# Gathering embedding rows straight into the residual tensor, five batches ahead

## The chip, the cores and the metric

One NeuronCore of a Trainium2 chip runs the whole program. The metric is device time in microseconds (us), the median of several runs. TensorE multiplies matrices, VectorE and ScalarE work on tiles, GpSimd does elementwise work and issues the indirect transfers (gathers and scatters by index), and SyncE issues plain transfers.

## The reference

The model is a small early-fusion network over a batch of 16. An image of 96 by 96 is cut into 36 patches and projected to 64 channels; 512 text tokens are looked up in a table of 50257 rows and get a position table added. The 548 tokens then pass four residual blocks, and only the text lookup is touched by this change:

```
h = patches(x) @ tok_W.T + tok_b                       # 16 x 36 x 64
h = concat([h, txt_W[x_txt] + pe], axis=1)             # 16 x 548 x 64
h = h + attn0(layernorm(h))     # relu attention, a two-layer FFN, layer norm
h = h + moe_top1(layernorm(h))  # gate, capacity, expert of 256 hidden units
h = h + attn1(layernorm(h))     # 16 heads of 4 channels, linear attention
h = h + moe_top2(layernorm(h))  # two of 8 experts
```

## The kernel before

Tokens lie on the 128 partitions, five slots of 128 a batch: slots 0 to 3 are the 512 text tokens, slot 4 the 36 image tokens. `H` (128 x 16 x 5 x 64, fp32, in SBUF) is the residual tensor of all 16 batches, and stays there for the whole program. The image slots of `H` are filled once, during the opening, by TensorE and ScalarE (L1070).

The first half of the program (up to the end of the gating of the first expert layer, about 350 us) is a software pipeline over batches. `for step in range(STEPS)` runs on every engine, with 25 steps, and a stage with lag k works on batch `step - k`:

```
LAG = dict(gather=0, norm1=1, cut1=2, qkv=3, attn=4, resid=5, ffn2=6, norm3=7, gate=8, scatter=9)
```

Each engine executes its own part of the step in a fixed order, written out by hand, and waits on semaphores in between; nothing reorders it at run time. What matters around the change:

- GpSimd, per step: `gather(b)` (four indirect transfers of 128 rows of 256 bytes each, L807, one for each text slot, into one of two staging tiles `emb`), then `low1` (L828, the low part of the split of the normalised tile), `offset` (L823, adds a bias row to `H[:, b]`), `scatter` (L815, five indirect transfers), and `low3` (L833). At step 10, ahead of the rest, stand two large subtractions of weights (L840). `gather(b)` from the third batch on waits until the addition that reads the staging tile of batch b - 2 is done.
- VectorE, per step: `norm1a(b)` waits for the gathers of its batch, adds the position table `pe` and writes `H[:, b, 0:4]` (L1307), then takes statistics (L1213, L1216). `norm1b(b)` (L1318 to L1322) normalises into the single tile `xt`, and for b >= 1 first waits for `low1(b-1)`, which reads `xt`. `late_weights(0)` (L1281 to L1295) prepares weights at step 3. `q_low` (L1330) and `k_low` (L1336) follow the projections.
- ScalarE: `roots1` (L1078, L1079) follows `norm1a`; `high1(b)` (L1085) follows `norm1b(b)` and releases `low1(b)`.
- TensorE: at step 3 it runs `moe_bias` (L997) and then `t1(0)` (L852), which waits for `low1(0)`; then the query projection (L862, L863), whose result `q_low(0)` reads before the key projection may begin.
- SyncE issues the weight loads and then 8 transfers of zeros into the scatter buffer, which keep the DMA engines full during the first 45 us.

So `low1(0)`, in step 2, comes behind the twelve gather instructions of steps 0, 1 and 2; `low1(1)` comes in step 3, and so on.

Of the kernel before, what the change touches and what calls it, by code (L numbers as in the profile page):

```python
# [9 lines left out]
ALU = mybir.AluOpType  # L10
# [4 lines left out]
P = 128  # L15
NB, N_IMG, N_TXT, D = 16, 36, 512, 64
# [3 lines left out]
TXT = N_TXT // P  # L20
# [19 lines left out]
PER = dict(norm1a=11, norm1b=4, qk_low=3, vals=1, resid=2, norm2a=12, norm2b=5, norm3a=10, norm3b=3, gate=6, place=7,  # L40
           mixed=12, weighted=5, norm4=5, kvnorm=3, fold=3, resid2=11, norm5=6, route_a=10, route_b=6)
# [37 lines left out]
def early_fusion_kernel(nc, i, out):  # L79
    with ExitStack() as ctx:  # L80
        def sb(name, shape, dt=F32):
            return ctx.enter_context(nc.sbuf_tensor(name, shape, dt))

        def pair(name, shape, dt=F32, depth=2):
            return [sb(f"{name}{k}", shape, dt) for k in range(depth)]
# [3 lines left out]
        def sem(name):  # L89
            if name not in sems:  # L90
                sems[name] = ctx.enter_context(nc.semaphore(name))
            return sems[name]
# [11 lines left out]
        H = sb("H", [P, NB, SLOTS, D])  # L104
# [8 lines left out]
        w = {}  # L113
# [17 lines left out]
        top_w, kept = sb("top_w", [P, NB, SLOTS]), sb("kept", [P, NB, SLOTS])  # L131
        carry = sb("carry", [P, E])

        emb = pair("emb", [P, TXT, D])
        stats = sb("stats", [P, SLOTS, 6])
        mv1, mv2, mv3 = (pair(f"mv{k}_", [P, SLOTS, 2]) for k in (1, 2, 3))
        sd1 = pair("sd1_", [P, 2, SLOTS])
# [33 lines left out]
        def bs(a, k):  # L171
            return a.unsqueeze(1).to_broadcast([a.shape[0], k, a.shape[1]])
# [13 lines left out]
        LAG = dict(gather=0, norm1=1, cut1=2, qkv=3, attn=4, resid=5, ffn2=6, norm3=7, gate=8, scatter=9)  # L186
        STEPS = NB + LAG["scatter"]
        WEIGHTS_STEP = 9

        def at(step, stage):  # L190
            b = step - LAG[stage]
            return b if 0 <= b < NB else None
# [96 lines left out]
        def pool_second(pool):  # L289
# [19 lines left out]
            def finish(b):  # L309

                for side, (_, _, s0, s1) in enumerate(PARTS):
                    pool.wait_ge(sem("weigh"), 2 * (POS * b + (side + 1) * E // 2))
                    h = H[:, b, s0:s1, :]
                    for k in range(2):
                        pool.tensor_tensor(h, h, acc[b % 2][:, s0:s1, k, :], ALU.add).then_inc(sem("finish"), 1)  # L315
                        pool.wait_ge(sem("finish"), 4 * b + 2 * side + k + 1)
# [24 lines left out]
        def pe_second(pe):  # L341
# [60 lines left out]
            def up(n, *tiles):  # L402

                b, side, p = unit(n)
                a, z, _, _ = PARTS[side]
                if n % POS == 0 and 0 in tiles:
                    pe.wait_ge(sem("xs5"), b + 1)
                for k in tiles:
                    j, e = k // 2, 2 * p + k % 2
                    m = up_bank(4 * n + k)  # L410
                    banks.take(pe, (m,), sem("gelu"), 4 * n + k + 1)
                    two(pe, bank(m)[:, 0:z - a], split["fw1"], xs2[b % 2][:, a:z], slice((e * J + j) * P, (e * J + j + 1) * P)).then_inc(sem("up"), 1)
# [356 lines left out]
        @block.sync  # L769
        def _(sp):  # L770
            for n in EARLY[:EARLY_BY_SP]:
                sp.dma_start(w[n][:], i[n]).then_inc(sem("early_in"), 16)
            sp.dma_start(fw1, i["fw1"]).then_inc(sem("middle_in"), 16)
            for n in MIDDLE:
                sp.dma_start(w[n][:], i[n]).then_inc(sem("middle_in"), 16)
            sp.dma_start(ew1, i["ew1"]).then_inc(sem("late_in"), 16)
            for n in LATE:
                sp.dma_start(w[n][:], i[n]).then_inc(sem("late_in"), 16)

            sp.wait_ge(sem("zero_set"), 1)  # L780
            for e in range(E):
                sp.dma_start(slots_buf[e * CP:(e + 1) * CP, :].rearrange("(p t) c -> p t c", p=P), zeros[:].unsqueeze(1).to_broadcast([P, ET, 2 * D])).then_inc(sem("slots_zeroed"), 16)
            for k in range(4):
                sp.wait_ge(sem(f"scattered{k}"), 16 * SLOTS * NB // 4)
            for e in range(E):
                if e >= 2:
                    sp.wait_ge(sem("b_turn"), UE * (e - 1))
                else:
                    sp.wait_ge(sem("low_w"), 2)
                sp.dma_start(xl[e % 2][:], slots_buf[e * CP:(e + 1) * CP, :].rearrange("(p t) c -> p t c", p=P)).then_inc(sem(f"xl_in{e % 2}"), 16)  # L790
                if e >= 2:
                    store_expert(sp, e - 2)
            store_expert(sp, E - 2)
            store_expert(sp, E - 1)
            outputs(sp)


        @block.gpsimd
        def _(pool):
            pool.dma_start(w["ids"][:], i["ids"]).then_inc(sem("ids_in"), 16)  # L800
            pool.wait_ge(sem("ids_in"), 16)

            def gather(b):
                if b >= 2:
                    pool.wait_ge(sem("norm1a"), (b - 2) * PER["norm1a"] + 1)
                for t in range(TXT):
                    pool.indirect_dma_start(emb[b % 2][:, t, :], None, i["table"], bass.IndirectOffsetOnAxis(w["ids"][:, b * TXT + t:b * TXT + t + 1], 0)).then_inc(sem(f"gathered{b % 2}"), 16)  # L807

            def scatter(b):
                if b == 0:  # L810
                    pool.wait_ge(sem("slots_zeroed"), 16 * E)
                pool.wait_ge(sem("place"), (b + 1) * PER["place"])
                for s in range(SLOTS):
                    rows = P if s < TXT else N_IMG
                    pool.indirect_dma_start(slots_buf, bass.IndirectOffsetOnAxis(slot_i[0:rows, b, s:s + 1], 0), hl3[b % 4][0:rows, s, :], None,  # L815
                                            bounds_check=E * CP - 1, oob_is_err=False).then_inc(sem(f"scattered{b % 4}"), 16)

            def offset(b):

                if b == 0:  # L820
                    pool.wait_ge(sem("prep"), 1)
                pool.wait_ge(sem("norm1b"), (b + 1) * PER["norm1b"])
                pool.tensor_tensor(H[:, b], H[:, b], bs(w["fb"][:], SLOTS), ALU.add).then_inc(sem("offset"), 1)  # L823

            def low1(b):
                pool.wait_ge(sem("high1"), b + 1)
                h = hl1[b % 2]
                pool.tensor_tensor(h[:, :, D:2 * D].bitcast(F32R), xt[:], h[:, :, 0:D], ALU.subtract).then_inc(sem("low1"), 1)  # L828

            def low3(b):  # L830
                pool.wait_ge(sem("high3"), b + 1)
                h = hl3[b % 4]
                pool.tensor_tensor(h[:, :, D:2 * D].bitcast(F32R), xt3[:], h[:, :, 0:D], ALU.subtract).then_inc(sem("low3"), 1)  # L833

            for step in range(STEPS):
                if step == WEIGHTS_STEP + 1:
                    pool.wait_ge(sem("high_w"), 2)
                    for name, src in (("ew1", ew1), ("fw1", fw1)):
                        hi, lo = split[name]
                        pool.tensor_tensor(lo[:], src, hi[:].bitcast(F32), ALU.subtract).then_inc(sem("low_w"), 1)  # L840
                for stage, f in (("gather", gather), ("cut1", low1), ("qkv", offset), ("scatter", scatter), ("norm3", low3)):
                    if (b := at(step, stage)) is not None:
                        f(b)
            pool_second(pool)
# [214 lines left out]
        def _(act):  # L1059
# [106 lines left out]
            for step in range(STEPS):  # L1166
                if step == WEIGHTS_STEP:

# [41 lines left out]
        def norm_stats(dve, st, src, mv):  # L1210

            for s in range(SLOTS):
                st(dve.bn_stats(stats[:, s, :], src[:, s, :]))  # L1213
            st.sync()
            for s in range(SLOTS):
                st(dve.bn_aggr(mv[:, s, :], stats[:, s, :]))  # L1216
# [8 lines left out]
        def _(dve):  # L1225
# [75 lines left out]

            def norm1a(b):
                st = Steps(dve, sem("norm1a"), "norm1a", b)
                dve.wait_ge(sem(f"gathered{b % 2}"), 16 * TXT * (b // 2 + 1))
                if b >= 2:
                    dve.wait_ge(sem("roots1"), b - 1)
                st(dve.tensor_tensor(H[:, b, 0:TXT, :], emb[b % 2][:], w["pe"][:], ALU.add))  # L1307
                st.sync()
                norm_stats(dve, st, H[:, b], mv1[b % 2])
                st.close()  # L1310
# [253 lines left out]
```

## Time and profile before

| | us |
|---|---|
| median of 3 runs | 995.72 |
| lowest and highest | 994.87, 998.15 |
| span of the profiled execution | 996.3 |

The profiled execution is 0.6 us above the median of the runs. In the profile PE is TensorE's matmuls, PEld its weight loads, DVE is VectorE, ACT ScalarE, POOL GpSimd and SP SyncE. Times are counted from the start of the span. A transfer that GpSimd issues shows as a busy stretch of GpSimd (the issuing work); the landing of its data is a separate time.

### The profile page before, as it was taken

How to read it: one execution, taken by the hardware profiler on the slowest of the kernel's cores; microseconds unless marked ns; L12 is line 12 of the kernel's file. 1: busy time of each engine (PE TensorE's matmuls, PEld its weight loads, DVE VectorE, ACT ScalarE, POOL GpSimd, SP SyncE). 2: the span in 40 equal slices, each digit the busy share in tenths (PEclk: the TensorE clock that was granted, in tenths of full speed). 3: DMA queues.
4: the chain of work that ended last, by engine and by line, in shares of the span. 5: the costliest groups of instructions: out<-in, count | busy, mean ns of one | idle time of the engine just before them, and what ended most of it. 6: DMA issues, size and time to landing. Idle time of an engine off the chain costs nothing.

```text
span 996.3 us, 17997 instructions
## 1 busy us (share of the span) xinstructions
PE 834.4 (84%) x5574; PEld 594.9 (60%) x5574; DVE 691.3 (69%) x2473; ACT 560.5 (56%) x1259; POOL 421.6 (42%) x441
## 2 busy tenths in 40 slices
PE   5799869999987549934589999999999999999995
PEld 3666646666664436614466676666766667666663
DVE  3758789898866525547767778787777777877542
ACT  1366635555543224412266767777777776777773
POOL 4554477674542620046635553455644453110110
PEclk9599879999986569965579999999999999999998
DMA  9700000000000023310000000000000000000000
GB/s 287 218 12 11 10 14 30 23 24 10 5 4 2 6 89 125 109 40 16 6 2 9 2 7 8 7 8 2 7 9 7 9 2 7 8 7 7 1 12 6
DMA packets 36328, 29.06 MB, mean 29 GB/s; under 512 B 18546, under 2 KB 31770, under 8 KB 35850
## 3 DMA queue, kind: packets, MB, share of 16 engines
q1 hardware_dynamic: 27226, 20.59, 6.8%
q0 software_dynamic: 7200, 5.16, 2.1%
q10 hardware_dynamic: 1808, 2.17, 0.6%
q8 instruction: 46, 0.75, 0.3%
q14 instruction: 48, 0.39, 0.1%
HBM read 16.23 MB, written 15.38 MB: 32 GB/s over the span
## 4 chain that ended last, share of the span: by engine, by line
PE 54%; DVE 8%; ACT 7%; issue 4%; DMA 0%; POOL 0%; ACTq 0%; POOLq 0%; DVEq 0%
PE psum L422 12%; PE psum L862 11%; PE psum L863 7%; PE psum L867 4%; PE psum L868 4%; PE psum L435 3%; PE psum L852 3%; PE psum L1039 2%; ACT L511 2%; ACT L464 1%; ACT scratch L511 1%; PE psum L1021 1%; PE psum L360 1%; DVE stats L1213 1%; PE psum L936 1%
## 5 line engine op out<-in xcount | busy, mean ns | idle before, releaser
L511 ACT ACTIVATE scratch<-psum,fb 128x292 f32<-128x292 f32 (+1 forms) x512 | 227.2, 490 | 51.3 <-PE psum L863 50.1
L862 PE MATMUL psum<-xs,fw_hi 128*128 128x292 f32 (+1 forms) x512 | 180.4, 362 | 27.7 <-ACT scratch L511 27.7
L862 PEld LDWEIGHTS psum<-xs,fw_hi 128*128 128x128 f32 x512 | 98.3, 192 | 88.2 <-ACT scratch L511 56.0
L422 PE MATMUL psum<-scratch,w_fw 128*64 128x292 f32 (+1 forms) x1024 | 148.6, 412 | 0.0
L863 PE MATMUL psum<-xs,fw_lo 128*128 128x292 f32 (+1 forms) x512 | 144.9, 293 | 0.0
L302 POOL DMA_INDIRECT uu<-expert_out,slot_i x80 | 84.1, 1051 | 68.7 <-DVE stats L1213 42.5
L852 PE MATMUL psum<-w_ident,hl 128*128 128x128 f32 (+1 forms) x400 | 72.9, 300 | 36.6 <-DVE hl L1222 26.3
L863 PEld LDWEIGHTS psum<-xs,fw_lo 128*128 128x128 f32 x512 | 99.6, 194 | 0.0
L815 POOL DMA_INDIRECT slots_buf<-hl,slot_i x80 | 79.7, 997 | 43.5 <-issue 26.3
L519 ACT ACTIVATE yt<-psum,w_fb 128x256 f32<-128x256 f32 (+1 forms) x128 | 62.6, 489 | 61.8 <-PE psum L422 61.8
L422 PEld LDWEIGHTS psum<-scratch,w_fw 128*64 128x64 f32 x1024 | 62.9, 138 | 42.6 <-issue 12.8
L852 PEld LDWEIGHTS psum<-w_ident,hl 128*128 128x128 f32 (+1 forms) x400 | 53.2, 155 | 57.6 <-issue 50.4
L1122 ACT ACTIVATE prob<-psum 128x256 f32<-128x256 f32 (+1 forms) x160 | 55.4, 397 | 49.5 <-PE psum L926 49.2
L807 POOL DMA_INDIRECT emb<-in_table,w_ids x64 | 62.7, 980 | 30.3 <-issue 16.1
L738 DVE TENSOR_TENSOR scratch<-psum,w 128x256 f32<-128x256 f32 (+1 forms) x96 | 46.6, 485 | 32.0 <-PE psum L435 27.6
L435 PE MATMUL psum<-w_ident,yt 128*128 128x128 f32 (+1 forms) x320 | 57.3, 277 | 5.8 <-DVE scratch L738 4.4
L315 POOL TENSOR_TENSOR H<-H,prob 128x128 f32<-128x128 f32 (+1 forms) x32 | 20.2, 631 | 96.0 <-DVE prob L740 94.7
L936 PE MATMUL psum<-prob,vv 128*64 128x256 f32 x320 | 59.5, 437 | 0.0
L925 PE MATMUL psum<-qst,kh 128*128 128x256 f32 (+1 forms) x160 | 54.0, 358 | 4.1 <-ACT prob L1122 3.7
L925 PEld LDWEIGHTS psum<-qst,kh 128*128 128x128 f32 x160 | 31.8, 199 | 41.5 <-issue 26.6
L315 POOL TENSOR_TENSOR H<-H,scratch 128x128 f32<-128x128 f32 (+1 forms) x32 | 18.4, 575 | 85.3 <-DVE scratch L740 84.0
L1213 DVE BATCH_NORM_STATS2 stats<-H 128x6 f32<-128x64 f32 x320 | 46.8, 213 | 2.2
(289 smaller groups left out, 1996.6 us busy)
## 6 DMA issues: line engine op xcount, KB each, us to landing
slots_buf<-zeros SPq DMA_DIRECT2D x8, 704.0 KB, 8.0
scratch<-slots_buf SPq DMA_DIRECT2D x8, 704.0 KB, 4.4
expert_out<-scratch SPq DMA_DIRECT2D x8, 352.0 KB, 2.5
out<-H SPq DMA_DIRECT2D x16, 128.0 KB
X<-in_patches ACTq DMA_DIRECT2D x1, 1728.0 KB, 7.8
slots_buf<-hl,slot_i POOLq DMA_INDIRECT x80
uu<-expert_out,slot_i POOLq DMA_INDIRECT x80, 2.3
scratch<-in_fw SPq DMA_DIRECT2D x1, 1024.0 KB
```

The source lines that it names most:

```text
L302: pool.indirect_dma_start(yg[b % 2][0:rows, s, :], None, expert_out, bass.IndirectOffsetOnAxis(slot_i[0:rows, b, s:s + 1], 0), bounds_chec ...
L422: last = pe.matmul(bank(6)[h * D:(h + 1) * D, 0:z - a], w["fw2"][:, (2 * p + h) * J + j, :], hid[(4 * n + 2 * j + h) % 8][:, 0:z - a], sta ...
L435: last = pe.transpose(bank(7)[0:rows, k:k + P], ysb[n % 2][:, k:k + rows], ident[:])
L511: act.activation(hid[m % 8][:, 0:z - a], bank(up_bank(m))[:, 0:z - a], ACT.Gelu, bias=fb1[:, e * J + j:e * J + j + 1]).then_inc(sem("gelu" ...
L519: act.activation(ysb[n % 2][:, 0:z - a], bank(6)[:, 0:z - a], ACT.Identity, bias=w["fb2"][:, p:p + 1]).then_inc(sem("ysb"), 1)
L807: pool.indirect_dma_start(emb[b % 2][:, t, :], None, i["table"], bass.IndirectOffsetOnAxis(w["ids"][:, b * TXT + t:b * TXT + t + 1], 0)).t ...
L815: pool.indirect_dma_start(slots_buf, bass.IndirectOffsetOnAxis(slot_i[0:rows, b, s:s + 1], 0), hl3[b % 4][0:rows, s, :], None, bounds_chec ...
L852: last = pe.transpose(bank(dst_bank, 2)[0:cols, s * P:s * P + rows], src[0:rows, s, :], ident[0:rows, 0:rows])
L862: pe.matmul(dst, parts[0][:, cols], rhs, start=True, stop=False)
L863: return pe.matmul(dst, parts[1][:, cols], rhs, start=False, stop=True)
L925: pe.matmul(dst, kh[b % 2][:, s * P:(s + 1) * P], qst[b % 2][:, a:z], start=True, stop=False)
L936: last = pe.matmul(bank(6)[h * D:(h + 1) * D, 0:z - a], vv[b % 2][:, s, :], prob[s][:, a:z], start=(s == 0), stop=(s == SLOTS - 1))
```

## The change

The staging pair `emb` is gone. Each gather writes its 128 rows straight into `H[:, b, t, :]`, and `norm1a(b)` adds the position table in place. Since nothing is reused, the gather waits for nothing but the index list, and every batch has a semaphore of its own. GpSimd issues the gathers of batches 0 to 4 ahead of its step loop, and in step s (ahead of the step's other GpSimd work, and from step 10 on behind the two large subtractions) the gather of batch s + 5, as long as there is one.

```
-        emb = pair("emb", [P, TXT, D])
...
+        AHEAD = 5
...
             def gather(b):
-                if b >= 2:
-                    pool.wait_ge(sem("norm1a"), (b - 2) * PER["norm1a"] + 1)
                 for t in range(TXT):
-                    pool.indirect_dma_start(emb[b % 2][:, t, :], None, i["table"], bass.IndirectOffsetOnAxis(w["ids"][:, b * TXT + t:b * TXT + t + 1], 0)).then_inc(sem(f"gathered{b % 2}"), 16)
+                    pool.indirect_dma_start(H[:, b, t, :], None, i["table"], bass.IndirectOffsetOnAxis(w["ids"][:, b * TXT + t:b * TXT + t + 1], 0)).then_inc(sem(f"gathered{b}"), 16)
...
+            for b in range(AHEAD):
+                gather(b)
             for step in range(STEPS):
                 if step == WEIGHTS_STEP + 1:
 ...
-                for stage, f in (("gather", gather), ("cut1", low1), ("qkv", offset), ("scatter", scatter), ("norm3", low3)):
+                if step + AHEAD < NB:
+                    gather(step + AHEAD)
+                for stage, f in (("cut1", low1), ("qkv", offset), ("scatter", scatter), ("norm3", low3)):
...
             def norm1a(b):
-                dve.wait_ge(sem(f"gathered{b % 2}"), 16 * TXT * (b // 2 + 1))
+                dve.wait_ge(sem(f"gathered{b}"), 16 * TXT)
...
-                st(dve.tensor_tensor(H[:, b, 0:TXT, :], emb[b % 2][:], w["pe"][:], ALU.add))
+                st(dve.tensor_tensor(H[:, b, 0:TXT, :], H[:, b, 0:TXT, :], w["pe"][:], ALU.add))
```

## Rows read from the trace of the kernel before

**Rows 1.** The page: span; engine's busy time, share; the gathers' busy us, mean ns.
```profile
span 996.3 us, 17997 instructions
...
PE 834.4 (84%) x5574; PEld 594.9 (60%) x5574; DVE 691.3 (69%) x2473; ACT 560.5 (56%) x1259; POOL 421.6 (42%) x441
...
L807 POOL DMA_INDIRECT emb<-in_table,w_ids x64 | 62.7, 980 | 30.3 <-issue 16.1
```

**Rows 2.** The chain of work that ended last, first piece listed: start, length, what.
```profile
254.56 0.08 issue
```

**Rows 3.** Timeline of GpSimd, opening: start, length, instruction, idle before it and releaser.
```profile
8.12 1.05 POOL L807 DMA_INDIRECT emb<-in_table,w_ids  x1 [6.03 <-DMA w_ids<-in_ids]
...
16.98 0.94 POOL L807 DMA_INDIRECT emb<-in_table,w_ids  x1 [0.30 <-issue]
22.77 0.94 POOL L807 DMA_INDIRECT emb<-in_table,w_ids  x1 [4.84 <-DVE stats L1213]
...
27.71 0.86 POOL L828 TENSOR_TENSOR hl<-xt,hl 128x320 fp32r<-128x320 f32 x1 [0.17 <-ACT hl L1085]
...
32.49 0.94 POOL L807 DMA_INDIRECT emb<-in_table,w_ids  x1 [0.30 <-issue]
33.58 0.94 POOL L828 TENSOR_TENSOR hl<-xt,hl 128x320 fp32r<-128x320 f32 x1
...
48.65 0.87 POOL L828 TENSOR_TENSOR hl<-xt,hl 128x320 fp32r<-128x320 f32 x1 [5.91 <-ACT hl L1085]
```

**Rows 4.** Timeline of VectorE, opening.
```profile
29.44 0.22 DVE L1318 RECIPROCAL rs<-sd 128x10 f32<-128x10 f32 x1 [0.56 <-ACT sd L1079]
...
36.52 0.79 DVE L1330 SCALAR_TENSOR_TENSOR qst<-psum,bq,qst 64x548 fp32r<-64x548 f32 x1
```

**Rows 5.** Timeline of TensorE, opening.
```profile
22.11 6.99 PE L997 MATMUL psum<-w_fln_b,scratch 64*128 64x1 f32 x32 [1.24 <-DVEq L1271]
29.03 1.36 PE L852 MATMUL psum<-w_ident,hl 128*128 128x128 f32 x5
...
37.37 0.60 PE L862 MATMUL psum<-xs,wk_hi 128*128 128x274 f32 x1 [4.98 <-DVE qst L1330]
...
44.70 0.43 PE L863 MATMUL psum<-xs,wq_lo 128*128 128x274 f32 x1
...
47.73 0.29 PE L863 MATMUL psum<-xs,wk_lo 128*128 128x274 f32 x1
```

**Rows 6.** The gathers' line: ns min/median/max of all 64; landings of the first 8, then 16.
```profile
L807 POOL DMA_INDIRECT emb<-in_table,w_ids x64: 938/947/1270, 8.1 to 227.0; - x64
...
DMA to landing us min/median/max: 6.1/6.2/6.5
...
DMA to landing us min/median/max: 2.3/3.4/5.0
```

**Rows 7.** Waits of GpSimd, whole span: us in total, times, longest.
```profile
POOL hl L828 <- ACT hl L1085: 64.2, 15, 7.7
...
POOL emb L807 <- DVE stats L1213: 7.5, 2, 4.8
```

**Rows 8.** Windows of one step each: length; PE, PEld, DVE, ACT, POOL busy; clock; DMA.
```profile
230.60:247.30 16.70, 15.46 (x110) 10.62 (x109) 14.94 (x65) 9.53 (x26) 7.65 (x9) 1.00 0.02 6
213.99:230.60 16.61, 15.41 (x109) 10.57 (x109) 14.85 (x65) 9.50 (x26) 11.49 (x12) 1.00 0.07 19
```

**Rows 9.** Timeline of GpSimd, `low1` at both ends of the window without gathers.
```profile
230.62 0.86 POOL L828 TENSOR_TENSOR hl<-xt,hl 128x320 fp32r<-128x320 f32 x1 [2.67 <-ACT hl L1085]
...
247.27 0.86 POOL L828 TENSOR_TENSOR hl<-xt,hl 128x320 fp32r<-128x320 f32 x1 [7.65 <-ACT hl L1085]
```

**Rows 10.** Windows of the opening, columns as in rows 8.
```profile
20.00:22.00 2.00, 0.87 (x10) 0.61 (x7) 0.54 (x4) 1.02 (x1) 0.00 (x0) 0.51 1.11 285
...
47.00:48.00 1.00, 1.00 (x8) 1.00 (x7) 0.93 (x4) 0.48 (x2) 0.00 (x0) 0.83 0.00 0
```

**Rows 11.** Waits of all engines, 60 to 130 us: the longest, none of them a DMA.
```profile
POOL hl L828 <- ACT hl L1085: 26.0, 5, 7.5
```

## The prediction

> **What bounds the kernel now.** I read the page first. GpSimd, the engine whose program is reordered, is busy for 42% of the 996.3 us [rows 1]. That says it is not the bound as a whole; what a change in its order is worth must be read from the stretches in which somebody waits for it. The chain of work that ended last comes next, but the pieces that the profile lists begin at 254.6 us [rows 2], after the last gather (the 64 gathers start between 8.1 and 227.0 us [rows 6]). So the chain doesn't cover the place of the change, and I go to the timelines of three engines over the opening and to the windows of single steps.
>
> The opening first. GpSimd issues eight gathers from 8.12 us, stands still for 4.84 us because the third batch must wait for the staging tile, issues four more, and runs `low1(0)` at 27.71 us, just when ScalarE's `high1(0)` is ready (0.17 us idle) [rows 3]. Three things hang on `low1(0)`. VectorE's `norm1b(1)` must not overwrite `xt` before it has been read; TensorE's `t1(0)` needs its output; and everything of batch 0 follows from `t1(0)`. In the trace `low1(0)` ends at 28.57 (27.71 + 0.86), `t1(0)` starts at 29.03 because TensorE is then done with `moe_bias`, and `norm1b(1)` starts at 29.44, released by ScalarE's roots [rows 3 to 5]. So GpSimd is now about level with its consumers: it leads `norm1b(1)` by 0.87 us and `t1(0)` by 0.46 us.
>
> From there on GpSimd is early. Of the 16 `low1`, 15 wait for ScalarE, 64.2 us in all [rows 7]; the only one that GpSimd itself holds back is `low1(1)` at 33.58 us, right behind a gather [rows 3], and its consumer on VectorE, `norm1b(2)`, comes after `q_low(0)`, which starts at 36.52 us [rows 4].
>
> Then the steady part. Steps last 16.6 us, with VectorE busy for 14.9 and TensorE for 15.4 of them [rows 8]. The window from 213.99 us holds four gathers (GpSimd busy 11.49 us), the one from 230.60 us holds none (7.65 us busy). Their lengths are 16.61 and 16.70 us, and VectorE's busy time 14.85 and 14.94 us. The reader is to see that the gathers of a step cost the step nothing: with them GpSimd waits 2.67 us for ScalarE ahead of `low1`, without them 7.65 us [rows 9]. The 5 us are idle time or gathers, as it happens.
>
> **The change, part by part.**
>
> The add in place (L1307) keeps its shape, type and number; only one input tile has another address. I take 0 us for it, 16 times. The gathers write the same 256 bytes a partition, into another tile: 0 us.
>
> The wait for the staging tile goes: 4.84 us of idle time ahead of the third batch, of which 0.30 would be there anyway [rows 3], so 4.54 us, plus a later one of 2.7 us (7.5 us in all [rows 7]), behind which GpSimd waits 5.91 us for ScalarE anyway [rows 3] and which is worth 0.
>
> The order is what costs. Before, the gathers of steps 0, 1 and 2 stand ahead of `low1(0)`: 12 instructions. After, the five batches ahead of the loop and those of steps 0, 1 and 2 stand ahead of it: 8 batches, 32 instructions. Each takes 0.95 us and a gap of 0.30, so 1.25 us from start to start (the first eight go from 8.12 to 16.98 us; the first two pitches are a little longer) [rows 3, 6]. The 8th stays at 16.98. The 32nd starts at 16.98 + 24 x 1.25 = 46.98 and ends at 47.92; `low1(0)` follows 0.15 us later, as `low1(1)` follows its gather now [rows 3], at 48.07, where it was 27.71: 20.4 us late. The same from the parts: 20 more gathers x 1.25 = 25.0, less 4.54, is 20.5.
>
> Who waits. `high1(0)` is ready at 27.6 as before, so all of it is GpSimd's. `low1(0)` ends at 48.93. `norm1b(1)` begins about 0.1 us later, 49.0 instead of 29.44: 19.6 us late, since the 0.87 us of lead are used up first. Behind it on VectorE, in order, stand `late_weights(0)` and `q_low(0)`; `q_low(0)` moves from 36.52 to 56.1, TensorE's key projection waits for it [rows 5], and with it scores, attention and everything of the later steps. `t1(0)` moves from 29.03 to about 49.1; its result is there long before `q_low(0)` comes round, as now (7 us between the end of `t1(0)` and `q_low(0)`), so it adds nothing.
>
> Is GpSimd late a second time? Step 3 holds the gather of batch 8 and then `low1(1)`: 48.93 + 5.2 = 54.1, 20.5 us later than before, for consumers that come after `q_low(0)` (56.1): covered. Step 4: `low1(1)` and `offset(0)` end at 55.9, four gathers end at 61.0, and `low1(2)`, now at 48.65 behind 5.91 us of waiting [rows 3], is wanted at 48.65 + 19.6 = 68.3: covered by 7 us. From there each step has its four gathers as before up to step 10, and the trace says that GpSimd waits in all of them. So the lateness stays at 19.6 us and isn't given back either, since from 60 to 130 us the engines wait for each other and for no transfer with a fixed date of its own [rows 11]; all of it moves together.
>
> Steps 11 to 15 lose their four gathers each: 20 x 1.25 = 25 us of GpSimd time. By the pair of windows their worth is 0 [rows 8, 9].
>
> The pitch of the gathers is the one price to bound. From below it is the 1.25 us seen. From above: the mean of the 64 is 0.980 us [rows 1], where the median is 0.947 [rows 6], and the longest is 1.270; 20 gathers at the mean add 0.7, and all 20 at the longest add 6.5 us (20 x (1.270 - 0.947)). The new ones run between 18 and 48 us, most of them while the other engines stand waiting, so I take half of the 0.7: 0.4 us. The DMA engines are full with loads and zeros (share 1.11 at 20 to 22 us [rows 10]); the first eight gathers land 6.1 to 6.5 us after issue, without growth from one to the next, the next 16 within 2.3 to 5.0 [rows 6], so the transfers keep up with a pitch of 1.25, and the first batch that VectorE still needs has landed 20 us ahead.
>
> Sum: 19.6 + 0.4 = 20.0 us. On the profiled span 996.3 gives 1016.3; the profiled execution is 0.6 above the median, so the median becomes 995.7 + 20.0 = **1015.7 us**.
>
> TensorE's clock. It fell to 1.2 GHz at 20 us (granted share 0.51 from 20 to 22 us, with TensorE busy for 0.87 us of the two), stood there, and came back to 2.4 GHz between 47 and 48 us, after dense matmuls since 37.4 [rows 5, 10]. The added 20 us of idle time fall in a stretch that is at 1.2 GHz anyway, and I expect the same 10 us of slow matmuls after it: 0 us. If the clock rises earlier or later against the work, matmuls change from 0.29 to 0.43 us [rows 5]; 10 us more or less of that is 10 x (1 - 0.29/0.43) = 3 us either way. Both ends stay in the range.
>
> **Rivals.**
>
> *The gathers were in the way in steps 11 to 15.* If GpSimd's order, or its use of the memory beside VectorE, set the length of those steps, taking out 20 gathers would give back up to 25 us against the 20 lost: 995.7 + 20.0 - 25.0 = 990.7 us, faster. It decides from 4 us a step, at which the loss is covered. For it speaks only that GpSimd, with gathers, is within 2.67 us of being late [rows 9]. Against it: the step without gathers is not shorter and VectorE is not less busy in it [rows 8]. The Trainium skill (Advanced Engine Details and Errata, VectorE Performance Modes, Mode Summary) has a rule on this side: VectorE's second port is shared with GpSimd, and the two block each other in its two-port modes. By that rule 20 gathers of 0.95 us less could free at most 19 us of VectorE's time, which would make about 997 us; this trace doesn't agree for the gathers, as VectorE's 14.85 and 14.94 us in the paired windows show.
>
> *The delay is swallowed.* If the pipeline, while it fills, caught up with something that has a date of its own (weights, zeros), the time would be 995.7 to 1000 us. Against it: no wait on a transfer between 60 and 130 us [rows 11], and 16.6 us a step afterwards whatever GpSimd does.
>
> *The gathers slow each other.* With 32 in a row against full DMA queues, GpSimd might be held at issue. With all 20 at the longest duration seen the sum is 19.6 + 6.5 = 26.1, the time 1021.8 us. Against it: the eighth in a row still takes 0.94 us [rows 3].
>
> **How the numbers follow.** The forecast has 0.86, the gathers slowing each other 0.07, the delay swallowed 0.04 (half of it within 0.3%), the gain in steps 11 to 15 0.03 (two thirds of it faster). A difference of 0.3%, 3 us, is about what a measurement can tell from no change here. So faster 0.02, same 0.03, slower 0.95. The range is the forecast with 3 us of clock either way and a little of the slower pitch: 1012.5 to 1019.5.
>
> **What would show it.** GpSimd should issue 32 gathers without a gap and run `low1(0)` at 48 us; VectorE's `norm1b(1)` should be released by it at about 49 us and `q_low(0)` start at 56; the key projection about 57; and `low1(2)` be released by ScalarE again, 19 to 21 us later than now. Steps 11 to 15 should still last 16.6 us, with GpSimd's wait ahead of `low1` at 7.6 us in place of 2.67. What would make me wrong: `low1(0)` well before 45 or after 50 us, a shorter step once the gathers are gone, or a stretch at 1.2 GHz later in the program that is longer or shorter by more than 10 us.

## The result, and the profile after

The changed kernel takes 1018.83 us (median of four runs, 1013.18 to 1021.98), the kernel before beside it 996.93 us (994.87 to 999.83). The medians are 21.9 us apart. The ratio, which is not taken from the two medians (their quotient is 1.0220), is 1.0204, with an interval from 1.0166 to 1.0242; on 996.93 us that is 20.3 us. The forecast was 1015.7 us, 20.0 us slower. Ratios, here and below, leave out the executions that ran well above the fastest of their kernel, among them one of 1243.21 and one of 3963.04 us. The profiled execution, at 1021.98 us, is the slowest of the four.

The page of the changed kernel, beside [rows 1]. GpSimd lines stand two lower than before, the lines behind them on the other engines two higher:
```profile
span 1020.2 us, 17997 instructions
...
PE 840.3 (82%) x5574; PEld 598.1 (59%) x5574; DVE 690.6 (68%) x2473; ACT 561.4 (55%) x1259; POOL 420.9 (41%) x441
...
L805 POOL DMA_INDIRECT H<-in_table,w_ids x64 | 62.0, 970 | 24.6 <-issue 17.4
```
The span grew by 23.9 us while every engine but TensorE is as busy as it was within 1 us, and TensorE is busy for 5.9 us more. So most of the loss is waiting, and a part is slower matmuls. The timeline of GpSimd over the opening, beside [rows 3]:
```profile
8.69 1.05 POOL L805 DMA_INDIRECT H<-in_table,w_ids  x1 [6.60 <-DMA w_ids<-in_ids]
...
17.55 0.94 POOL L805 DMA_INDIRECT H<-in_table,w_ids  x1 [0.30 <-issue]
...
47.69 0.94 POOL L805 DMA_INDIRECT H<-in_table,w_ids  x1 [0.30 <-issue]
48.75 0.86 POOL L826 TENSOR_TENSOR hl<-xt,hl 128x320 fp32r<-128x320 f32 x1
...
68.91 0.87 POOL L826 TENSOR_TENSOR hl<-xt,hl 128x320 fp32r<-128x320 f32 x1 [7.79 <-ACT hl L1087]
```
The 32 gathers run without a gap. From the 8th to the 32nd (17.55 to 47.69) there are 24 pitches in 30.14 us, 1.256 each. `low1(0)`, the first 128x320 subtraction, follows with no wait of its own at 48.75 instead of 27.71. The first gather is 0.57 us later than before because the list of indices landed later in this execution. `low1(2)` is released by ScalarE again. The two consumers, beside [rows 4] and [rows 5], VectorE first:
```profile
49.75 0.22 DVE L1320 RECIPROCAL rs<-sd 128x10 f32<-128x10 f32 x1 [19.42 <-POOL hl L826]
...
57.02 0.80 DVE L1332 SCALAR_TENSOR_TENSOR qst<-psum,bq,qst 64x548 fp32r<-64x548 f32 x1
```
TensorE:
```profile
49.67 1.36 PE L854 MATMUL psum<-w_ident,hl 128*128 128x128 f32 x5 [19.20 <-POOL hl L826]
...
57.87 0.60 PE L864 MATMUL psum<-xs,wk_hi 128*128 128x274 f32 x1 [4.84 <-DVE qst L1332]
```
Both now wait some 19 us for `low1(0)`; before, neither waited for GpSimd. `norm1b(1)` starts 20.31 us later than in [rows 4] (49.75 less 29.44), `q_low(0)` 20.5.

Windows of one step each, beside [rows 8] (columns as there), without gathers in both: the first two lines. The third is a window around step 9 in the changed kernel:
```profile
221.80:238.50 16.70, 15.48 (x110) 10.64 (x109) 14.92 (x65) 9.56 (x26) 7.60 (x9) 1.00 0.06 18
238.50:255.10 16.60, 15.40 (x110) 10.56 (x109) 14.84 (x65) 9.50 (x26) 7.56 (x9) 1.00 0.04 12
134.00:158.00 24.00, 24.00 (x101) 16.66 (x100) 14.86 (x46) 9.59 (x25) 11.38 (x9) 0.51 0.05 14
```
Steps without gathers last 16.6 to 16.7 us, as those with four gathers did in the kernel before. GpSimd waits 7.6 us ahead of `low1` in them, as the start of the first window shows:
```profile
221.86 0.86 POOL L826 TENSOR_TENSOR hl<-xt,hl 128x320 fp32r<-128x320 f32 x1 [7.66 <-ACT hl L1087]
```

How much later than before the same instruction starts, along the program, from the starts of `low1`, `low3` and a share instruction of the second half in both traces:
```
after the opening   low1 of batches 2 to 7        +20.3 to 20.4 us
after step 9        low1 of batches 8 to 15       +24.0 to 24.5
from 288 to 306 us  last low3                     +20.1, then 19.5
expert stage ends   434.38 before, 453.79 after   +19.4
second half         16 share instructions         +18.8 to 25.3, last 23.9
```
The opening alone gives 20.3 of the 23.9 us. The rest comes and goes with stretches at 1.2 GHz: in the third window above the granted share is 0.51 throughout, where the kernel before, 20.3 us earlier in its program, had 13.7 us at 2.4 GHz in the middle (its row comes with the last experiment); from 293 to 303 us it was the kernel before that had such a stretch, and 5 us come back there; and short ones in the second half (before: three, after: five, of 3 to 7 us each) leave a net 4.4 us.

### The profile page after: what moved, and what is told of

It reads as the page before. It is cut to its first block, busy times and chain, and to the rows that moved or that the text cites. A ratio compares the mean times of both kernels' runs of the same rounds, so it can differ in the third digit from the quotient of the medians.

```text
span 1020.2 us, 17997 instructions
## 1 busy us (share of the span) xinstructions
PE 840.3 (82%) x5574; PEld 598.1 (59%) x5574; DVE 690.6 (68%) x2473; ACT 561.4 (55%) x1259; POOL 420.9 (41%) x441
## 4 chain that ended last, share of the span: by engine, by line
PE 53%; DVE 8%; ACT 6%; issue 4%; DMA 0%; POOL 0%; ACTq 0%; POOLq 0%; DVEq 0%
PE psum L422 12%; PE psum L864 11%; PE psum L865 7%; PE psum L869 4%; PE psum L870 4%; PE psum L435 3%; PE psum L854 3%; PE psum L1041 2%; ACT L511 2%; ACT L464 1%; ACT scratch L511 1%; PE psum L360 1%; PE psum L1023 1%; DVE stats L1215 1%; DVE zt L1379 1%
## 5 line engine op out<-in xcount | busy, mean ns | idle before, releaser
L864 PE MATMUL psum<-xs,fw_hi 128*128 128x292 f32 (+1 forms) x512 | 181.6, 364 | 27.7 <-ACT scratch L511 27.7
L854 PE MATMUL psum<-w_ident,hl 128*128 128x128 f32 (+1 forms) x400 | 72.4, 298 | 56.3 <-DVE hl L1224 26.8
L805 POOL DMA_INDIRECT H<-in_table,w_ids x64 | 62.0, 970 | 24.6 <-issue 17.4
L315 POOL TENSOR_TENSOR H<-H,prob 128x128 f32<-128x128 f32 (+1 forms) x32 | 20.2, 631 | 96.0 <-DVE prob L740 94.7
L826 POOL TENSOR_TENSOR hl<-xt,hl 128x320 fp32r<-128x320 f32 x16 | 13.8, 863 | 91.2 <-ACT hl L1087 91.0
```

What stands on the lines that cost most here:

```text
L805: pool.indirect_dma_start(H[:, b, t, :], None, i["table"], bass.IndirectOffsetOnAxis(w["ids"][:, b * TXT + t:b * TXT + t + 1], 0)).then_in ...
L854: last = pe.transpose(bank(dst_bank, 2)[0:cols, s * P:s * P + rows], src[0:rows, s, :], ident[0:rows, 0:rows])
L864: pe.matmul(dst, parts[0][:, cols], rhs, start=True, stop=False)
```

## The experiments

Twelve runs, the changed kernel and the one before once more among them, on four chips. The medians of the kernel before are 1027.5 us on chip A (the changed kernel again, none ahead, the order alone, the first run with two ahead), 1011.0 on chip B, 996.8 on chip C and 1014.3 on chip D, against 996.93 in the first pair. So every ratio is against the kernel before on the same chip. The theories: the loss is the number of gathers ahead of `low1(0)` (order); or it is the destination, the add in place and the dropped wait; or, for the differences in size, TensorE's clock.

**The changed kernel again, and the same with no batch ahead** (`AHEAD = 0`; the gathers go straight into `H`, the order is the old one, the wait is gone).

> The changed kernel once more, to size the loss. My theory has two parts: 20.3 us from the order of GpSimd's work in the opening, the same in every execution, and on top of it stretches at 1.2 GHz that fall elsewhere from execution to execution (+4.2 us in step 9, back again near 290 us, +4.5 us in the second half of the first profile). So low1(0) starts at 48.1 to 48.8 us and ScalarE's high1 of the third to the eighth batch is 20 us later than before in this profile as well, while what comes behind 130 us moves by 17 to 25 us; median 1014 to 1020. Rival: the extra is a fixed cost of the change in step 9 and in the second half (23 to 24 us at the end in this profile too, with the same places).

> The changed kernel with AHEAD = 0: gathers straight into the residual tensor, add in place, no wait for a staging tile, but in the order of before (12 gathers ahead of low1(0)). Order theory: low1(0) back at 27.7 us (it waits for ScalarE's high1 then) and the time within 3 us of the kernel before. Rival, the destination or the add in place costs something: the time stays above before by what they cost, up to 20 us, and L1309 (the add) takes longer than 0.42 us.

Measured: again 1.0216 (1.017 to 1.0261), the medians 23.7 us apart. With no batch ahead 1.0014 (0.9981 to 1.0047), the medians 2.7 us apart: the loss is gone. But the openings are not the expected ones. The timeline of ScalarE, changed kernel, chip A:
```profile
54.62 1.02 ACT L1072 ACTIVATE H<-psum 36x1024 f32<-36x1024 f32 x1 [33.03 <-remote]
```
and that of GpSimd:
```profile
47.36 0.95 POOL L805 DMA_INDIRECT H<-in_table,w_ids  x1 [0.30 <-issue]
...
61.41 0.86 POOL L826 TENSOR_TENSOR hl<-xt,hl 128x320 fp32r<-128x320 f32 x1 [13.11 <-ACT hl L1087]
```
The image rows, which ScalarE copies out of PSUM into `H`, are needed by the first add and all behind it. TensorE has them done at 23.53 by its records; in the first profile of the changed kernel ScalarE took them at 22.29. Here it takes them at 54.62, 6.3 us after the last gather of the burst has ended (48.31). "remote" says that no instruction's record accounts for the release at that time. The 32 gathers themselves go at the same pitch as ever. With no batch ahead, on GpSimd:
```profile
33.94 0.86 POOL L826 TENSOR_TENSOR hl<-xt,hl 128x320 fp32r<-128x320 f32 x1 [10.82 <-ACT hl L1087]
```
`low1(0)` was expected at 27.7. Some 1.5 us of the difference are the patches' transfer, which landed later (the patch product is done at 18.60, in the first trace of before at 17.13). The 12 gathers, now without the break for the staging tile, end at 23.12. Here it is an earlier signal that comes late: ScalarE goes on from the patch product at 22.91. TensorE, which waits for that, turns the image rows only at 25.14; ScalarE copies them into `H` at 27.06, and `low1(0)` is behind them. So here the dropped wait gained nothing in the opening.

**The order alone.** The gathers in the new order, into memory other than `H`, and added from there as before:
```diff
+        emb = pair("emb", [P, TXT, D])
...
+        def staged(b):
+            return emb[b][:] if b < 2 else X[:, b, 0:TXT, :]
...
             def gather(b):
+                if b == 2:
+                    pool.wait_ge(sem("patch_prod"), 1)
...
-                    pool.indirect_dma_start(H[:, b, t, :], None, i["table"], ...
+                    pool.indirect_dma_start(staged(b)[:, t, :], None, i["table"], ...
...
-                st(dve.tensor_tensor(H[:, b, 0:TXT, :], H[:, b, 0:TXT, :], w["pe"][:], ALU.add))
+                st(dve.tensor_tensor(H[:, b, 0:TXT, :], staged(b), w["pe"][:], ALU.add))
```

> The other half alone: the order of the changed kernel (five batches ahead, 32 gathers ahead of low1(0)), but the rows land in a staging place (the old pair of tiles for the first two batches, the not yet used residual copy X for the others) and the add reads from there. The third batch waits for the patch matmuls, which end at 17 us, so for nothing. Order theory: low1(0) at 48 to 49 us, time within 3 us of the changed kernel (1013 to 1021). Rival, the loss is the destination's or the in-place add's: near 997.

Measured: 1.0181 (1.0131 to 1.0232), which is 18.6 us on 1027.5, the medians 22.3 us apart; `low1(0)` at 50.17. The order alone makes the loss. GpSimd:
```profile
20.05 0.95 POOL L811 DMA_INDIRECT X<-in_table,w_ids  x1 [2.08 <-PE psum L885]
...
50.17 0.88 POOL L832 TENSOR_TENSOR hl<-xt,hl 128x320 fp32r<-128x320 f32 x1
```
This kernel has a break of 2.08 us behind the eighth gather, in which GpSimd waits for the patch product. ScalarE took the image rows, done at 24.00, at 25.93, with gathers running again for 5.9 us, on the chip on which the changed kernel took them at 54.62. The late signal shows up one place further on: `t1(0)` ends at 52.46 (51.10 + 1.36), and ScalarE takes its result at 60.19, 4.2 us after the last of the four gathers of batch 8, the one at 55.05, has ended (56.0).

**Two batches ahead** (`AHEAD = 2`), three times.

> The changed kernel with AHEAD = 2, so 20 gathers ahead of low1(0) where it has 12 before and 32 after. Order theory with 1.25 us for each: the 20th gather ends at 8.1 + 19 x 1.25 + 1.0 = 32.9 us, low1(0) starts at 33.1, 5.4 us later than before, and 0.9 us of that is lead that is used up: 4.5 us slower than before, about 1001. Rival, any run ahead costs the same (the burst as such): about 1018. Rival, a delay of a few us is swallowed while the pipeline fills: within 1.5 us of before.

> AHEAD = 2 once more, whose profile was disturbed and which took 14 us more than before where 4.5 were expected. If GpSimd's order alone sets the opening, low1(0) starts at 33.1 us, 5.4 us later than before, and the kernel is 4.5 us slower. If late signals behind the burst set it, low1(0) waits for ScalarE, some 10 us behind the 20th gather (44 us), and the kernel is 10 to 14 us slower.

> AHEAD = 2 a third time, since its first two runs were on chips whose TensorE signals came late. On a chip whose signals are prompt (first add at 22 to 24 us) the order theory says: 20 gathers ahead of low1(0), which starts at 33.1 us, 5.4 us later than before; 0.9 of it is lead; 4.5 us slower than before, ratio 1.003 to 1.006. Rival, a short delay is swallowed while the pipeline fills: ratio within 1.001. On a chip with late signals: the first add at 36 us or later, low1(0) near 44, ratio 1.010 to 1.016 again.

Measured: 1.0138 (1.0096 to 1.018), 1.0137 (1.0059 to 1.0215) and 1.0118 (1.0064 to 1.0173), that is 12 to 14 us (the medians are 14.9, 15.5 and 11.6 us apart) where 4.5 were expected of the count alone. The profiled execution of the first is the one of 1243.21 us; of it only the opening is used. `low1(0)` stood at 44.40, 43.88 and 44.12, not at 33.1. The third, ScalarE and then GpSimd:
```profile
37.33 1.02 ACT L1072 ACTIVATE H<-psum 36x1024 f32<-36x1024 f32 x1 [16.59 <-remote]
```
```profile
32.39 0.94 POOL L805 DMA_INDIRECT H<-in_table,w_ids  x1 [0.30 <-issue]
...
44.12 0.86 POOL L826 TENSOR_TENSOR hl<-xt,hl 128x320 fp32r<-128x320 f32 x1 [10.79 <-ACT hl L1087]
```
The burst of 20 gathers ends at 33.33, the image rows follow 4.0 us later. All three runs have late signals, so what two batches ahead cost where signals are prompt wasn't measured.

**The kernel before again**, on chip B.

> The kernel before once more, for its profile on the chip of these runs, since the first four experiments took some 30 us more than the first pair, with stretches in the opening in which ScalarE or VectorE went on long after the TensorE instruction they wait for had ended (up to 33 us). Theory: the kernel before has such stretches too, and they end a few us after GpSimd's burst of gathers ends (12 gathers, so near 25 to 35 us), low1(0) then starts at 32 to 36 us instead of 27.7. Rival: the stretches are the changed kernel's alone, and low1(0) starts at 27.7 us here as well.

Measured: two executions, 1005.88 and 1022.45 us, the second profiled; of it only the opening is used. Image rows at 21.06, `low1(0)` at 28.80, 1.1 us later than in [rows 3]. So the expectation that the kernel before has such late signals as well, with `low1(0)` at 32 to 36 us, failed. GpSimd:
```profile
23.85 0.94 POOL L807 DMA_INDIRECT emb<-in_table,w_ids  x1 [5.30 <-DVE stats L1213]
...
28.80 0.86 POOL L828 TENSOR_TENSOR hl<-xt,hl 128x320 fp32r<-128x320 f32 x1 [0.17 <-ACT hl L1085]
```
The wait for the staging tile makes a break of 5.30 us after eight gathers, and the image rows are done (21.03) and read inside it. The patch product was read at once too (done at 17.49, taken at 17.59), while the first eight gathers were being issued.

**A later place for each gather.** Three batches ahead, and from there each gather behind its step's own GpSimd work:
```diff
-        AHEAD = 5
+        AHEAD = 3
...
-                if step + AHEAD < NB:
-                    gather(step + AHEAD)
...
+                if 2 <= step <= NB - 2:
+                    gather(step + 1)
```

> Rows straight into the residual tensor, but never ahead of work that is waited for: the first three batches are gathered ahead of the loop (12 gathers ahead of low1(0), as before), each later batch behind the step's own GpSimd work, two steps ahead of its add. Order theory: low1(0) at 27.7 us, low1(1) about 28.8 instead of 33.6, no other wait, and the time within 2 us of the kernel before, since norm1b(2) has 7 us to spare. Rival, the changed kernel's loss is in the run ahead as such or in the destination: slower than before by 3 us or more.

Measured: 1.0073 (1.0029 to 1.0117), the medians 5.0 us apart where at most 2 were expected. Again 12 gathers stand ahead of `low1(0)`, without a break; they end at 23.29; ScalarE goes on from the patch product (done at 18.85) at 25.47, takes the image rows at 29.63, and `low1(0)` starts at 36.43 (28.80 in the kernel before on this chip, where the patch product was done 1.4 us earlier). A third of the changed kernel's ratio for 12 gathers instead of 32.

**TensorE kept busy in the stall**, to price the clock:
```diff
+            def keep_busy(n):
+                for _ in range(n):
+                    pe.matmul(bank(4)[:, 0:TXT * D], ident[:], w["pe"][:].rearrange("p t c -> p (t c)"), start=True, stop=True)
...
                     moe_bias(pe)
+                    keep_busy(N_WAIT)
...
+                    if step == LAG["qkv"] and s == 1:
+                        keep_busy(N_GAP)
```
with 30 and 5 matmuls whose result nobody uses.

> The changed kernel with TensorE kept busy while it waits for low1(0): 30 matmuls of the identity with the position table into a free bank behind moe_bias, and 5 between the first query and key projections (their results are read by nobody). It tells what the clock of the opening is worth. Forecast in the prediction: 9.8 us at 1.2 GHz behind the stall are worth at most 3 us. So the clock should stand at 2.4 GHz from about 40 us, and the kernel be 0 to 3 us faster than the changed one (18 to 22 us slower than before). Rival, the idle time of TensorE costs more than the delay itself: faster than the changed kernel by 5 us or more. If the filling matmuls last longer than the wait, t1(0) starts later than 49.7 us and the kernel is slower.

Measured: 1.041 (1.0348 to 1.0473), the medians 41.1 us apart, and no answer. `moe_bias` itself came only at 54.78, 1.2 us behind the late image rows (53.58), so the added matmuls ran not in the stall but behind it. TensorE:
```profile
61.70 14.73 PE L1005 MATMUL psum<-w_pe,w_ident 128*128 128x256 f32 x60
76.27 0.78 PE L855 MATMUL psum<-w_ident,hl 128*128 128x128 f32 x5
```
They delayed `t1(0)` to 76.27. What the 1.2 GHz of the opening is worth stays open.

**The old order and the old wait, into `H`.** With no batch ahead, plus
```diff
             def gather(b):
+                if b >= 2:
+                    pool.wait_ge(sem("norm1a"), (b - 2) * PER["norm1a"] + 1)
```

> AHEAD = 0 with the old wait put back in (the gather of batch b waits for the add of batch b - 2), so that only the destination, the add in place and the semaphores differ from before. Theory from the runs so far: on the chips where TensorE's signals come late, they come only when GpSimd's unbroken burst of gathers has landed, and the wait behind the eighth gather was the break that let them through. Then the first add starts within 1 us of where it starts before (23.2 us in the last profile of before; 28.3 with AHEAD = 0), low1(0) near 28.8, and the time within 3 us of before. Rival, the late signals have nothing to do with the burst's length: the first add at 28 us or later, as with AHEAD = 0.

Measured, on chip C: 0.9991 (0.9969 to 1.0014). The destination, the add in place (420 ns at the median, 418 in the kernel before) and the semaphores of their own for each batch cost nothing. The break is back as well, and the first add starts at 22.56 (expected within 1 us of 23.2). But this run can't tell whether the break lets the signals through: no kernel without the break and with the zeros in their old place ran on chip C. GpSimd:
```profile
23.25 0.94 POOL L807 DMA_INDIRECT H<-in_table,w_ids  x1 [5.29 <-DVE stats L1217]
...
28.20 0.86 POOL L828 TENSOR_TENSOR hl<-xt,hl 128x320 fp32r<-128x320 f32 x1 [0.17 <-ACT hl L1089]
```

**The zeros later**, in the changed kernel and in the one before, to see whether the zeros, which with the loads fill the queues in the opening, make the signals late. In the first trace of before the DMA engines are full until some 42 us rather than 45 (share 1.07 from 30 to 40 us, 0.53 from 40 to 45):
```diff
             sp.wait_ge(sem("zero_set"), 1)
+            sp.wait_ge(sem("attend"), SLOTS)
```

> The changed kernel, with SyncE's eight transfers of zeros issued only once the first batch's attention is done (they are needed by the first scatter, at step 9). Theory A, TensorE's signals are late because the many completion signals of gathers and zeros together are in their way: without the zeros image rows reach the residual tensor at 22 to 25 us as in the very first profile of the changed kernel (54.6 us in its second), low1(0) starts at 48 to 49 us, and the kernel is 17 to 21 us slower than before. Theory B, the gathers alone are enough: ScalarE's copy of the image rows still waits until some 4 us behind the end of the burst (52 us or later), low1(0) at 58 us or later.

> The kernel before with the zeros issued late in the same way. Under theory A it gains where TensorE's signals are late in the opening: 1 to 5 us; under theory B, and on a chip whose signals are prompt, within 3 us of before, since the zeros lie beside everything else either way. It gets slower only if the gathers or the first scatter then wait for the zeros (they should have landed by 100 us, 20 us ahead of the scatter).

Measured, on chip C: 1.017 (1.0133 to 1.0207), the medians 17.6 us apart, and 0.999 (0.997 to 1.001). The zeros cost nothing in their old place. The image rows come promptly, as expected if the zeros were what makes signals late. But the two are not told apart: chip C may be prompt anyway, as the first pair's chip was with the zeros in place (the kernel before takes 996.8 us here and 996.93 there), and the changed kernel with its zeros in place wasn't run on chip C. ScalarE, GpSimd and VectorE of the changed kernel with late zeros:
```profile
21.11 1.02 ACT L1073 ACTIVATE H<-psum 36x1024 f32<-36x1024 f32 x1 [1.79 <-PE psum L891]
```
```profile
48.23 0.86 POOL L827 TENSOR_TENSOR hl<-xt,hl 128x320 fp32r<-128x320 f32 x1
```
```profile
49.22 0.22 DVE L1321 RECIPROCAL rs<-sd 128x10 f32<-128x10 f32 x1 [20.14 <-POOL hl L827]
```
That is the forecast opening (48.07 and 49.0) to 0.2 us. And its lateness against the first trace of before is 20.0 us from there through the whole pipeline. In the window in which the changed kernel's first profile lost 4.2 us, the kernel before and then this one:
```profile
119.00:132.70 13.70, 11.00 (x83) 8.01 (x82) 12.94 (x41) 6.76 (x19) 10.86 (x9) 1.00 0.07 22
```
```profile
139.10:152.70 13.60, 10.93 (x83) 7.93 (x81) 12.82 (x41) 6.76 (x19) 10.86 (x9) 1.00 0.07 22
```
The same 83 matmuls take the same 11 us at 2.4 GHz, 20 us later. So the changed order doesn't bring the 1.2 GHz at that place by itself.

## Why the prediction was right, step by step

**The count of gathers.** Right, and shown: 32 instead of 12 stand ahead of `low1(0)`. With the count back at 12 and the wait kept the ratio is 0.9991; with the new order and nothing else of the change 1.0181. The pitch was 1.256 us where 1.25 + 0.02 (the 0.4 us over 20) was taken: over 24 pitches that is 0.14 us more than 1.25 gives, where 0.4 was added.

**Who waits.** Right. `norm1b(1)` and `t1(0)` are released by `low1(0)`. The lateness at `norm1b(1)` is 20.31 us, and less the 0.57 us of the later index list 19.74, against 19.6 + 0.4. (The 7 us said to lie between the end of `t1(0)` and `q_low(0)` are 6.1 in [rows 4] and [rows 5] and 6.0 afterwards; nothing hangs on it.)

**GpSimd isn't late a second time, and nothing is swallowed.** Right: `low1(2)` waits 7.79 us for ScalarE and 14 of the 16 `low1` wait for it, 91.0 us in all (64.2 before, [rows 7]). Of the 26.8 us more, 26.0 are in steps 11 to 15, where `low1` waits 7.65 us instead of 1.6 to 2.7: the time of the gathers that went to the front, now idle.

**Steps 11 to 15.** Right: 16.6 to 16.7 us with no gather in them, 16.61 before with four [rows 8]. The rival that would have made the kernel faster asked for shorter steps or a less busy VectorE; VectorE is busy for 14.84 to 14.92 us a step, as before. The rule of the Trainium skill (Advanced Engine Details and Errata, VectorE Performance Modes, Mode Summary) that VectorE's second port is shared with GpSimd, so that the two block each other in VectorE's two-port modes, doesn't show in the gathers here: taking them out freed none of VectorE's time.

**The dropped wait.** The 4.54 us that the forecast credits to its removal hold where signals are prompt: in the first profile and on chip C the 32 gathers run through, and on chip C the opening comes out to 0.2 us. On other chips the step failed. On chips A and B, 12 gathers without the break bring `low1(0)` not to 27.7 but to 33.94 and 36.43, where the kernel before, with its break, has it at 28.80 on chip B. The prediction costed the wait as idle time of GpSimd alone. That the first pair ran where signals are prompt is luck.

**The clock.** Forecast 0 with 3 us either way. Measured in the first profile +4.2, -5.0 and +4.4 us in three places, in the zeros-late profile none of the three (19.9 to 20.1 us late in the first half from `low1(2)` on, 20.2 at the last share instruction). Each of the three is larger than the 3 us allowed, and so is their sum, 3.6; that the first two nearly cancel is luck. That this is scatter between executions fits the four of the changed kernel: the three of 1018.66 to 1021.98 us have a mean granted clock of 0.885 or 0.886, the one of 1013.18 us 0.894. It lies behind the difference between 20.3 us at the opening and 23.9 at the end of the profiled one. The stall itself did fall in a stretch at 1.2 GHz, as forecast: 20.0 to 47.3 us before, 21.7 to 66.1 after. Whether a clock kept at 2.4 GHz would give some of it back wasn't settled.

The medians of the changed order lie 17.6 to 23.7 us above before in four runs (the first pair, two on chip A, one on chip C). On the chips with late signals part of that is another mechanism than the forecast: `low1(0)` at 61.41 instead of 48.75 on chip A, with the total no worse than +23.7, so some of those 12.7 us come back or are in the slower kernel before as well (its profile on chip A wasn't taken).

No kernel here beats the one before: the best are 0.9991 and 0.999, with 1 in both intervals.

## What to carry to other kernels

A prefetch on an in-order queue is paid for by whatever stands behind it: count the instructions ahead of the first one that others wait for, times the issue pitch, less the lead it has now. Here the zeros in the DMA queues cost nothing beside it. Taking work out of steps in which its engine already waits for another gains nothing, so a run ahead should be no longer than the first consumer allows. And a wait that looks like idle time of its engine may stand beside something that its removal changes: price the removal from a trace without it.

## What the runs showed that wasn't expected

In the traces of chips A, B and D TensorE's results often reach the other engines late while GpSimd issues gathers without a break; in the first pair and on chip C they don't. All from the traces: how many gathers the burst has and when its last one ends, when the matmuls are done by their records, and when the engine that waits for them goes on.
```
                                      chip  gathers  ends    matmuls done  reader goes on
image rows, changed kernel             A      32     48.31      23.53         54.62
image rows, changed, busy TensorE      B      32     47.86      22.39         53.58
image rows, two ahead (first)          A      20     33.83      23.92         37.60
image rows, two ahead (second)         B      20     33.14      21.90         37.08
image rows, two ahead (third)          D      20     33.33      22.45         37.33
biases, changed kernel                 A      32     48.31      18.41         31.15
biases, two ahead (third)              D      20     33.33      18.79         25.63
patch product, none ahead              A      12     23.12      18.60         22.91
patch product, later place             B      12     23.29      18.85         25.47
biases, before (break)                 B       8     18.55      18.29         20.55
image rows, before (break)             B       8     18.55      21.03         21.06
image rows, order alone (break)        A       8     17.97      24.00         25.93
image rows, changed, first profile     -      32     48.63      22.26         22.29
image rows, changed, late zeros        C      32     48.10      21.08         21.11
```
On chips A, B and D the image rows, given in the middle of a burst of 20 or 32, are read 3.8 to 4.0 us after the end of one of 20 and 5.7 or 6.3 us after one of 32. A signal given earlier is read 4 to 13 us late, inside the burst or, once, 2.2 us behind it. In the two traces with a break after eight gathers (5.30 and 2.08 us) the image rows were read 0.03 and 1.9 us after they were done, but the second reading lies in the burst behind the break. So it is not shown that a break is what lets signals through. GpSimd's own pitch doesn't change. What holds the signals back, the gathers' own completion signals, those of the zeros or something else, and what differs between the chips, stays open: the run that was to tell, with the zeros late, came out prompt on a chip where the same kernel with its zeros in place wasn't run.

Nor was it expected that the stretches at 1.2 GHz stand in other places from one profile to the next, with the same order of work (only the zeros differ): the changed kernel's first profile has one from 134 to 159 us and short ones at 557, 591, 718, 748 and 905, the one with late zeros has 2.4 GHz from 140 to 152 and short ones at 559, 777 and 808. Each such difference was worth 4 to 5 us of this span.
